# Scan phase of a conv and state-space hybrid: the output slab summed in PSUM through an identity product, copied back by ScalarE, and the carried columns copied three at a time

## What is computed

```python
xs = jnp.stack([x1, x2], axis=1)                     # rows, columns
xs = jnp.concatenate([xs, xs[..., ::-1]], axis=1)    # and both backwards
delta = softplus(dts + dt_b)
dA, dBu = exp(delta * A), delta * Bs * xs
h = dA * h + dBu                                     # 8 states, 96 channels, 4096 steps
y = einsum('bkdn,bkn->bkd', h, c) + Ds * xs
ysum = y1 + inv[:, 0] + wh + invwh                   # the four directions, added back in place
yo = layernorm(ysum, ln_g, ln_b) * silu(z)
```

## Time and profile before

| | us |
|---|---|
| median of the runs | 7660.85 |
| span of the profiled execution | 7664.9 |
| scan phase: first and last scan of L1543 near | 3250 and 6330 |
| busy VectorE / TensorE / GpSimd / ScalarE, whole span | 6472.2 / 6122.8 / 5465.9 / 5261.8 |
| mean granted TensorE clock | 0.883 |

### The profile page before, as it was taken

One profiled execution on the slowest core, in us unless ns is written; L12 is line 12 of the kernel. 1 busy time (PEld: TensorE's weight loads), 2 busy tenths in 40 slices (PEclk: granted clock), 3 DMA queues, 4 the chain that ended last, 5 costly groups with the idle time before them and its releaser, 6 DMA issues. The chain is left out here.

```text
span 7664.9 us, 105037 instructions
## 1 busy us (share of the span) xinstructions
PE 6122.8 (80%) x18336; PEld 2135.9 (28%) x18336; DVE 6472.2 (84%) x7490; ACT 5261.8 (69%) x10936; POOL 5465.9 (71%) x4289
## 2 busy tenths in 40 slices
PE   7887888888878885488888888888888777888686
PEld 2222222222222221122222222222222113488242
DVE  6999999999999997299999999999999994623636
ACT  6777777777777774377777777777777774322746
POOL 5888888888888885088888888888888881000606
PEclk8998899998898897688999999999999887997888
DMA  4444444544444445388888888888888873256322
GB/s 91 109 104 99 100 100 107 111 102 100 103 109 109 100 100 115 105 188 181 185 186 187 187 187 187 188 186 185 185 185 185 185 172 93 94 159 189 85 65 76
DMA packets 580313, 1051.07 MB, mean 137 GB/s; under 512 B 101639, under 2 KB 136636, under 8 KB 575004
## 3 DMA queue, kind: packets, MB, share of 16 engines
q1 hardware_dynamic: 579964, 1047.69, 58.3%
HBM read 857.89 MB, written 189.54 MB: 137 GB/s over the span
## 5 line engine op out<-in xcount | busy, mean ns | idle before, releaser
L1619 POOL TENSOR_TENSOR scan_prod<-scan_hs,scan_BC_rep 128x512 f32<-128x512 f32 x1536 | 1940.9, 1271 | 319.2 <-DVE scan_hs L1543 309.4
L639 POOL TENSOR_TENSOR mamba_prod<-mamba_hs,mamba_BC_rep 128x512 f32<-128x512 f32 x1536 | 1922.5, 1271 | 303.1 <-DVE mamba_hs L597 261.5
L597 DVE TENSOR_TENSOR_SCAN mamba_hs<-mamba_dA,mamba_carry,mamba_dbx 128x512 f32<-128x512 f32 x1152 | 1464.0, 1271 | 0.0
L1168 PE MATMUL scan_u_rep<-scan_du,scan_sel 96*128 96x512 f32 x1536 | 940.1, 696 | 524.1 <-DVE scan_hs L1543 523.4
L522 ACT ACTIVATE mamba_dA<-mamba_delta_rep,mamba_a_neg 128x512 f32<-128x512 f32 x1536 | 1090.1, 711 | 217.7 <-DVE mamba_hs L597 165.8
L1393 ACT ACTIVATE scan_dA<-scan_delta_rep,scan_a_neg 128x512 f32<-128x512 f32 x1536 | 1092.4, 712 | 91.0 <-DVE scan_hs L1543 80.7
L1543 DVE TENSOR_TENSOR_SCAN scan_hs<-scan_dA,scan_carry,scan_dbx_even 128x512 f32<-128x512 f32 x768 | 975.1, 1270 | 46.3 <-ACT scan_carry L1373 26.8
L1543 DVE TENSOR_TENSOR_SCAN scan_hs<-scan_dA,scan_carry,scan_u_rep 128x512 f32<-128x512 f32 x768 | 975.8, 1271 | 40.8 <-ACT scan_carry L1373 37.1
L577 DVE TENSOR_TENSOR mamba_dbx<-mamba_u_rep,mamba_BC_rep 128x512 f32<-128x512 f32 x1152 | 787.7, 684 | 199.4 <-DMA mamba_BC_rep<-bc_units 103.8
L321 PE MATMUL mamba_u_rep<-mamba_du,mamba_sel 96*128 96x512 f32 x768 | 484.0, 715 | 478.9 <-DVE mamba_hs L597 478.2
L1942 POOL TENSOR_TENSOR ffn_sq<-ffn_xm 96x512 f32<-96x512 f32 x64 | 66.2, 1034 | 961.5 <-DVE ffn_xm L1910 951.2
(11 more groups left out here) (283 smaller groups left out, 10550.4 us busy)
## 6 DMA issues: line engine op xcount, KB each, us to landing
scan_BC_rep<-proj_rows SPq DMA_DIRECT2D x1024, 256.0 KB, 6.5
scan_delta_rep<-proj_rows SPq DMA_DIRECT2D x1024, 192.0 KB, 3.6
mamba_BC_rep<-bc_units SPq DMA_DIRECT2D x256, 512.0 KB, 10.6
mamba_delta_rep<-delta_units SPq DMA_DIRECT2D x512, 192.0 KB, 3.7
proj_rows<-scan_dbc SPq DMA_DIRECT2D x256, 224.0 KB, 3.5
delta_units<-mamba_delta SPq DMA_DIRECT2D x128, 192.0 KB, 6.9
by_n<-fin_res SPq DMA_DIRECT2D x32, 768.0 KB, 3.2
fmid_src<-by_n SPq DMA_DIRECT2D x32, 768.0 KB, 5.2
```

Source lines behind the costliest of these rows:

```text
L597: nc.vector.tensor_tensor_scan(hs[:, s % RING_H], dA[:, s % RING_A], dbx_bank(s)[:], carry[:, bass.ds(at, 1)], op0=ALU.mult, op1=ALU.add). ...
L639: pool.tensor_tensor(prod[:, (G * u + s) % RING_P], hs[:, s % RING_H], BC_rep[:, u, QUADS + s % QUADS], ALU.mult).then_inc(s_prod, 1)
L1168: nc.tensor.matmul(u_rep[c][:], sel[:, c], du[:, k], start=True, stop=True).then_inc(s_rep_u, 1)
L1619: pool.tensor_tensor(prod[:, (G * k + s) % RING_P], hs[:, (G * k + s) % RING_H], BC_rep[:, k, 2 + s % 2], ALU.mult).then_inc(s_prod, 1)
```

## The change

Three edits, all in `ss2d_phase`.

1. `accumulate` is gone from VectorE. `sum_half` now begins a unit with a product of `ident` (96 x 96) and the unit's slab of Y, `start=True`, and the six gather products add to it. The product first waits for `s_acc` (the slab before has been copied back) and `s_yinit`.
2. ScalarE copies the bank back over the slab, `evict_y`, at s = 1 of the unit two after it, behind `dA`.
3. `carry_states` copies 3 columns at s = 0 and s = 3 (groups q-6 to q-4) instead of one per group; the scan's wait on `s_carry` is counted in these batches.

```diff
-            def sum_half(j, k, i):
+            def sum_half(j, k, i, image, r, started):
                 if i == 0:
                     wait(pe, s_acc, j)
+                    pe.wait_ge(s_yinit, started)
+                    nc.tensor.matmul(split(y[:]), ident[:], by_direction(Y, image, r, k), start=True, stop=False)
                 pe.wait_ge(s_prod, G * j + G - 1 + i)
                 for c in range(BLOCKS):
                     last = nc.tensor.matmul(y[32 * c:32 * c + 32], gather[:], prod[:, (G * k + 2 * c + i) % RING_P],
-                                            start=(i == 0), stop=(i == 1))
+                                            start=False, stop=(i == 1))
...
-            def carry_state(g, to):
+            def carry_states(g, to):
                 end = 0 if g // G >= 2 else T - 1
-                nc.scalar.activation(carry[:, bass.ds(to + g, 1)], hs[:, g % RING_H, end:end + 1], ACT.Copy
+                at = g % RING_H
+                nc.scalar.activation(carry[:, bass.ds(to + g, BATCH)], hs[:, at:at + BATCH, end], ACT.Copy
                                      ).then_inc(s_carry, 1)
+            def evict_y(j, k, image, r):
+                act.wait_ge(s_red, 2 * (j + 1))
+                nc.scalar.activation(by_direction(Y, image, r, k), split(y[:]), ACT.Copy).then_inc(s_acc, 1)
...
-                        if at >= RING_A:
-                            carry_state(at - RING_A, carried)
-                        elif not first:
-                            carry_state(GC + at - RING_A, carried_before)
+                        if s % BATCH == 0:
+                            if at >= 2 * BATCH:
+                                carry_states(at - 2 * BATCH, carried)
+                            elif not first:
+                                carry_states(GC + at - 2 * BATCH, carried_before)
+                        if s == 1 and k >= 2:
+                            evict_y(j - 2, k - 2, *now)
+                        if s == 1 and k < 2 and not first:
+                            evict_y(j - 2, k + 2, *before)
...
-            def accumulate(j, k, image, r, started):
-                dve.wait_ge(s_red, 2 * (j + 1))
-                dve.wait_ge(s_yinit, started)
-                wait(dve, s_acc, j)
-                Yv = by_direction(Y, image, r, k)
-                nc.vector.tensor_tensor(Yv, Yv, split(y[:]), ALU.add).then_inc(s_acc, 1)
...
-                        wait(dve, s_carry, q - RING_H + 1)
+                        wait(dve, s_carry, G // BATCH * (j - 1) + s // BATCH + 1)
...
-                        if s == ACC and k:
-                            accumulate(j - 1, k - 1, *now, started)
-                        if s == ACC and not k and prev:
-                            accumulate(j - 1, D - 1, *prev, began)
```

More of the change, by code:

```diff
@@ L868, in ss2d_phase @@
     RING_P = 12
-    ACC = 5
+    BATCH = 3
     CONV_TAPS = {2: (0, 1), 3: (1, 3), 4: (3, 4), 5: (4, 6), 6: (6, 7), 7: (7, 9)}
-    RING_A = 4
     with nc.cleanup_on_exit(), ExitStack() as ctx:
@@ L1184, in body @@
                 nxt = values(pe, (n + 1) // CH % 2, (n + 1) % CH, ((n + 1) // CH + 1) * CH) if has_next else None
+                if not (isinstance(n, int) and n == 0):
+                    before = values(pe, (n - 1) // CH % 2, (n - 1) % CH, ((n - 1) // CH + 1) * CH)
                 if has_out:
@@ L1227, in body @@
                         if s in (1, 2) and not (isinstance(n, int) and n == 0 and k == 0):
-                            sum_half(j - 1, (k + D - 1) % D, s - 1)
+                            sum_half(j - 1, (k + D - 1) % D, s - 1, *(now if k else before))
             for v in range(2):
@@ L1251, in _ @@
             for i in range(2):
-                sum_half(D * NC - 1, D - 1, i)
+                sum_half(D * NC - 1, D - 1, i, (NC - 1) // CH % 2, CH - 1, NC)
             pe.wait_ge(s_acc, D * NC)
@@ L1383, in body @@
                 carried_before = None if first else values(act, ((n - 1) % CH + 1) * GC)[0]
+                now = values(act, n // CH % 2, n % CH)
+                before = None if first else values(act, (n - 1) // CH % 2, (n - 1) % CH)
                 for k in range(D):
@@ L1442, in _ @@
             bodies(act, body)
+            for k in (D - 2, D - 1):
+                evict_y(D * (NC - 1) + k, k, (NC - 1) // CH % 2, CH - 1)
             act.wait_ge(s_scan, GROUPS)
@@ L1521, in body @@
                 has_next = nxt_lay is not None
-                now = values(dve, n // CH % 2, n % CH)
-                started = values(dve, (n // CH + 1) * CH)[0]
-                if isinstance(n, int) and n == 0:
-                    prev, began = None, None
-                else:
-                    prev = values(dve, (n - 1) // CH % 2, (n - 1) % CH)
-                    began = values(dve, ((n - 1) // CH + 1) * CH)[0]
                 at = values(dve, n % CH * GC)[0]
@@ L1545, in body @@
                                                      op0=ALU.mult, op1=ALU.add).then_inc(s_scan, 1)
-                        if s == ACC and k:
-                            accumulate(j - 1, k - 1, *now, started)
-                        if s == ACC and not k and prev:
-                            accumulate(j - 1, D - 1, *prev, began)
             times_b(0, 0, 0)
             bodies(dve, body)
-            accumulate(D * NC - 1, D - 1, (NC - 1) // CH % 2, CH - 1, NC)
             dve.wait_ge(s_scan, GROUPS)
```

## The result

The changed kernel takes **7772.39 us** (median of 4 runs, 7753.07 to 7779.45) against 7663.70 for the kernel before in the same session: ratio 1.0131, 95% interval 1.0118 to 1.0145, 1.3% slower. (The quotient of the two medians is 1.0142. The profiled execution spans 7773.0 us, 108.1 more than before.

What follows compares the result with a forecast made beforehand. It took TensorE's chains through ScalarE and GpSimd, not VectorE, to bound most rounds, and SP the last ones. Terms of +6, +14, 0 and +1 made +21, rounded to +18 on 7660.85: 7679 us, range 7600 to 7755.

Steps and rivals of the forecast that it cites:

- of its 1.8 us nothing is seen: First half: VectorE loses 3.5 us a round, 1.8 in each half, but TensorE's chain decides, so none of it shows here.
- It adds 1.7 us: First half: the identity product of k = 3, read down the columns, stands before taps and projection and lengthens the chain 1.7 us.
- First half: 25.1 us: Scan 1 to scan 13: 23.57 us before, plus 1.7 for the identity product, less 0.2 for column copies.
- The sign that was named for this half: Scan 13 waits 3 to 4 us in rounds 8 to 55, for the Exp behind ScalarE's wait for the projection.
- Second half: 22.8 us: Scan 13 to next scan 1, rounds 8 to 39: 22.8 us through softplus, gate, output product and copy; 23.7 in scan b.
- those of k = 1 and 2 fall in TensorE's idle time: TensorE: these identity products fit into idle time, such as the 2.76 us ahead of 4245.33.
- so this half gains 0.6 to 1.9: Second half: shorter by 0.6 to 1.9 us, 1.3 taken; the difference in the earlier trace was TensorE at half rate.
- The sum: All rounds: +6 us in rounds 8 to 39, +14 in 40 to 55, +1 for last slabs: +21, rounded to +18.
- Rounds 56 to 63 at SP's pace: Rounds without taps: SP is the bound at 48.30 us a round, since row stores wait to land; change 0.
- Rival 1: TensorE falls to its lower clock at the first chain's start: +62 us, 7741 in all; chance 0.37 with smaller mishaps.
- TensorE has 5 us more work, so fewer gaps: Argument against rival 1's lower clock: 5 us more TensorE work leaves fewer gaps.
- Rival 2: Fuller TensorE keeps 2.4 GHz and the half rate at 4245 and 5022 goes: -49 us, 7612 in all; chance 0.17.

Runs made afterwards that it cites:

- the run along rows: The changed kernel with every identity product reading its slab along rows, also for k = 1 and 3 (wrong part of the slab): 7700.95 us, ratio 1.0041 to the kernel before.
- four other kernels: Product added at s = 0 to: VectorE adds 1, 3 (7685.85 us); before with batched carries (7646.91); before (7663.32); VectorE adds 2, 3 (7696.25).
- the hybrid `(0, 3)`: The changed kernel, but VectorE adds the sums of k = 0 and 3 as before: 7716.32 us, ratio 1.0071 to the kernel before.
- the two rows alone: The changed kernel, but VectorE adds k = 1 and 3 as before; only k = 0 and 2 go the new way: 7731.75 us, ratio 1.0079 to the kernel before.

## Why the prediction was wrong, step by step

Two steps failed, and both priced TensorE's work at 2.4 GHz wherever it stands. The first half was reckoned without a fall of the clock (25.1 us; the means were 26.17 and 25.84), and the second half had the products of k = 1 and 2 in idle time where they cannot run (22.8 us; the mean was 24.30). The parts:

- **VectorE's 3.5 us a round and "of its 1.8 us nothing is seen"**: right. Without the additions the kernel gains 34 us of 225.
- **"It adds 1.7 us", the product of k = 3 down the columns**: right, 1.87 to 1.88 us a product, and 25.12 - 23.40 = 1.7 in the round. The Trainium skill ("TensorE: Matmul & The Clock Gate", Back-to-back issue gap) gives the gap between products by the columns streamed, with no term for their layout; by it both layouts would cost the same. The rows (1.02 and 1.88) and the run along rows speak against it here.
- **Carries -0.2, copy of the slab +0.5 - 0.27**: right within what the runs resolve (-11 us and +6 us in all). A copy down the columns takes 1.06 us, inside the bounds 0.5 to 1.27, and where ScalarE waits anyway.
- **The size of a group**: 24 x 1.78 is 42.7, not 42.5, so the forecast's own waits are 1.6 us a round, as its two rows (0.46 and 1.17) add up to. The forecast does not rest on it.
- **"First half: 25.1 us"**: this step failed as a mean. It holds in rounds at 2.4 GHz and is the shortest of rounds 8 to 55; the means were 26.17 and 25.84. The term left out of the sum, the fall to 1.2 GHz behind the wait of 1.2 us, is 1.3 us in a round that has it. Against 25.1 the means are 34 us more in rounds 8 to 39 and 12 in 40 to 55. The sign that was named for this half failed too: scan 13 waits 1.63 to 1.78 us in each of the 48 rounds, not 3 to 4, and the larger wait is that of scan 10 (mean 2.75), whose Exp stands behind the same projection.
- **"Second half: 22.8 us"**: this failed more. The best rounds have 23.07, and the means were 24.30 (scan a, +48 us against 22.8) and 24.53 (scan b, +13 against 23.7). The sentence that failed is "those of k = 1 and 2 fall in TensorE's idle time": no product can run in that idle time, since each stands behind the u product that waits for the scan. They stand behind the gap, at the rate that follows it, ahead of the variance and the output product. And "so this half gains 0.6 to 1.9" counted on the half rate of the earlier trace rows going away. It moved instead: over rounds 8 to 55 the u product of k = 3 takes 1.30 us in the mean (before 1.53), that of k = 2 takes 1.55 (before 1.35).
- **The sum**: +21 for the rounds, and 34 + 12 + 48 + 13 = 107 not in it. The base was off too: rounds 8 to 55 of before really took means of 47.79 and 48.72, so that the forecast's 47.9 and 48.8 are only 5 us above them, not 20. 5 + 107 = 112, less the 9 us that rounds 0 to 7 and 56 to 62 gave (forecast 0), is the +103 of the table; 5 more lie outside these rounds.
- **Rounds 56 to 63 at SP's pace**: 47.29 instead of 48.28, a little gained, and single rounds of 44.36 and 44.97 show that SP's 48.30 bounds no single round. In rounds 40 to 55 the loop through SP seems to hold the faster kernels: every version under 7670 us takes 48.7 to 49.4 a round there, 48.72 before. Without additions and with batched carries VectorE waits from 5200 to 5900 above all for rows from DRAM (waits: us, times, longest):

```profile
DVE scan_dbx_even L1511 <- DMA scan_BC_rep<-proj_rows: 57.1, 39, 3.5
```

- **Rival 1** (lower clock at the start of the first chain, 7741, chance 0.37) was right that the clock falls in the first chain, wrong in where and in what it costs. Its sign, a u product of over 1.3 us in most rounds, came in one round of 48 (2.07 in round 9); the clock falls behind the u product, at the sum and the tap. Its 1.3 us a round were 0.8 for the half rate as before, averaged over the rounds, and 0.5 for a longer identity product; but the identity product takes 1.87 to 1.91 us at either rate. That sum and tap lose 1.3 us too (0.87 and 0.45, in a round that has the fall) is a coincidence. It reckoned 62 us more for the first half, which lost 46 against the forecast, and it lacked the other two places.
- **"TensorE has 5 us more work, so fewer gaps"**, for which the forecast was preferred: true of the whole and not of the places that matter. Before the u products, TensorE waits 316.3 us for scans in all, before 523.4:

```profile
L1167 PE MATMUL scan_u_rep<-scan_du,scan_sel 96*128 96x512 f32 x1536 | 885.9, 667 | 316.8 <-DVE scan_hs L1546 316.3
L1168 PE MATMUL scan_u_rep<-scan_du,scan_sel 96*128 96x512 f32 x1536 | 940.1, 696 | 524.1 <-DVE scan_hs L1543 523.4
```

(The second row is of the kernel before.) But the wait in front of the first chain grew, over rounds 8 to 55, from 0.80 to 0.94 us in the mean, and that at k = 2 from 0.92 to 1.05; the one at k = 3 shrank from 2.63 to 1.81 and still stands before falls. They are waits for scans, and a slower chain makes scans later.
- **Rival 2** rests on a rule of the Trainium skill ("TensorE: Matmul & The Clock Gate", Part 1: activity releases the throttle). These traces agree in part. The product added at s = 0 of the changed kernel took the half rate from the first sum in all 48 rounds; the identity products at s = 1, behind the wait, did not. In four other kernels products added at s = 0 gave 0.0055 and 0.0032, nothing that shows, and a loss of 0.0044.

What stays open: which waits bring a fall, since 1.16 us does not in one kernel and 0.66 does in another; and why one program stays for ten rounds and more in a rhythm with falls in each, and then leaves it. The runs show that it happens, and that the period repeats to 0.01 us, not what ends it. How much of the second half's loss is the clock and how much the places of the products was not separated either. A sum that reads the right part of the slab along rows in all directions (from a second slab in transposed order) was not tried.

## What to carry to other kernels

Moving work from the busiest engine to one with idle time does not help where that idle time stands in front of a chain that others wait for and the work comes behind it; ask where in its queue the new instruction stands, and which wait it stands behind. A clock that falls behind such a wait can nearly double what a product takes (1.02 against 1.91 us here), so try a part of the edit at the place with slack before the whole: here the edit on three of four units costs nothing (0.9981, with the carries alone 0.9986), on all four it loses 1.3%, and on the two rows alone 0.8%, so the parts do not simply add up. And when rounds of different content last the same time to 0.01 us, look for a rhythm in the clock and not in the work.

## What I had not expected of the hardware

- A product whose moving side is read down the columns takes 1.88 us at 2.4 GHz (5318.69) and 1.91 at 1.2 GHz (4578.81): the lower clock costs it almost nothing. One along rows does feel the clock. The identity products of k = 0 and k = 2 in round 26 of the changed kernel:

```profile
4568.00 1.02 PE L1175 MATMUL scan_y<-scan_Y,scan_ident 96*96 x2
...
4590.60 1.91 PE L1175 MATMUL scan_y<-scan_Y,scan_ident 96*96 x2
```

- Rounds 25 to 29 of the changed kernel and rounds 12 to 15 of the hybrid `(0, 3)` all last 51.20 us, though their halves differ (26.43 and 24.77; 26.41 and 24.79) and the hybrid has two products fewer. So the length does not come from the amount of work alone. Both have a half rate at the same three places, at or behind the u products of s = 1 of k = 0, 2 and 3; the one of k = 0 in the hybrid:

```profile
3838.94 2.08 PE L1169 MATMUL scan_u_rep<-scan_du,scan_sel 96*128 96x512 f32 x2 [1.19 <-DVE scan_hs L1563]
3840.95 1.93 PE L1181 MATMUL scan_y<-scan_prod,scan_gather 128*32 128x512 f32 x6
```
